# Merging two work streams on a NeuronCore: the hand-out tables of all four compute engines replaced

## What is computed

```python
x = x + ssm(layernorm(x))     # gated state-space layer, 8 heads, with a rotation of the state
x = x + ffn(layernorm(x))     # 256 -> 2 x 1024 -> 1024 -> 1024 -> 256
x = x + delta(layernorm(x))   # delta-rule attention, 8 heads of 32, scan over the tokens
x = x + ffn(layernorm(x))     # the same weights as the first

def ffn(x):
    h = silu((x @ w1.T) * s1) * ((x @ w2.T) * s2)
    h = gelu((h @ h1.T) * sh1)
    h = gelu((h @ h2.T) * sh2)
    return (h @ w3.T) * s3
```

## Time and profile before

| | us |
|---|---|
| median of 3 runs | 2490.34 |
| lowest and highest run | 2489.7, 2496.93 |
| the profiled execution | 2494.62 |
| its span in the trace | 2492.6 |

### The profile page before, as it was taken

One profiled execution on the slowest core, in us unless ns is written; L12 is line 12 of the kernel. 1 busy time (PEld: TensorE's weight loads), 2 busy tenths in 40 slices (PEclk: granted clock), 3 DMA queues, 4 the chain that ended last, 5 costly groups with the idle time before them and its releaser, 6 DMA issues.

```text
span 2492.6 us, 60186 instructions
## 1 busy us (share of the span) xinstructions
PE 2245.7 (90%) x24704; PEld 1963.5 (79%) x24704; DVE 1221.2 (49%) x3186; ACT 1102.8 (44%) x2169; POOL 804.7 (32%) x873
## 2 busy tenths in 40 slices
PE   5798985897999989999999989999899999899888
PEld 3577974676888878887788878888798888888788
DVE  4546344455635654355534656346543655434431
ACT  3465431363435733365333654356342664333233
POOL 3222331322333233332333333332332333233233
PEclk8799997898999999999999999999999999999999
DMA  8000001000010001000010000100010000000000
GB/s 258 1 1 1 1 6 29 4 1 3 17 36 2 1 11 39 7 1 2 19 34 4 1 2 18 36 2 1 7 40 10 1 1 18 25 4 19 18 11 9
DMA packets 85456, 43.69 MB, mean 18 GB/s; under 512 B 69936, under 2 KB 80048, under 8 KB 85168
## 3 DMA queue, kind: packets, MB, share of 16 engines
q1 hardware_dynamic: 81504, 28.11, 4.6%
q0 software_dynamic: 3664, 11.53, 1.4%
HBM read 27.05 MB, written 12.58 MB: 16 GB/s over the span
## 4 chain that ended last, share of the span: by engine, by line
PE 55%; issue 16%; DVE 14%; POOL 9%; ACT 3%; DMA 1%; SPq 0%; DVEq 0%; POOLq 0%; ACTq 0%
PE F L1336 23%; PE Q L1395 5%; PE F L1315 5%; POOL hA_lo L604 4%; PE Q L1465 2%; PE F L1358 2%; PE Q L1429 2%; DVE hid L976 2%; POOL hB_lo L604 2%; PE Q L1448 2%; POOL rn L660 2%; DVE Q L1176 2%; DVE ti L1178 2%; PE Q L1433 1%; PE Q L1407 1%
## 5 line engine op out<-in xcount | busy, mean ns | idle before, releaser
L604 POOL TENSOR_TENSOR hA_lo<-hid,hA_hi 128x512 fp32r<-128x512 f32 x256 | 333.4, 1303 | 660.4 <-ACT hA_hi L741 348.0
L1336 PE MATMUL F<-hB_hi,h_sb 128*128 128x256 f32 x2048 | 499.7, 286 | 6.4 <-POOL hB_lo L604 6.4
L1336 PE MATMUL F<-hA_hi,h_sb 128*128 128x256 f32 x2048 | 500.8, 287 | 4.2 <-POOL hA_lo L604 4.2
L1336 PE MATMUL F<-hA_lo,h_sb 128*128 128x256 f32 x2048 | 487.5, 280 | 4.8 <-issue 4.8
L1336 PE MATMUL F<-hB_lo,h_sb 128*128 128x256 f32 x2048 | 488.4, 280 | 0.0
L1336 PEld LDWEIGHTS F<-hB_hi,h_sb 128*128 128x128 f32 x2048 | 387.2, 189 | 16.1 <-POOL hB_lo L604 8.8
L1336 PEld LDWEIGHTS F<-hA_hi,h_sb 128*128 128x128 f32 x2048 | 386.5, 189 | 13.2 <-POOL hA_lo L604 6.4
L1336 PEld LDWEIGHTS F<-hA_lo,h_sb 128*128 128x128 f32 x2048 | 387.1, 189 | 6.9 <-issue 6.6
L1336 PEld LDWEIGHTS F<-hB_lo,h_sb 128*128 128x128 f32 x2048 | 387.9, 189 | 0.0
L1315 PE MATMUL F<-xf_hi,w_sb 128*128 128x256 f32 x1024 | 275.3, 305 | 39.3 <-DVEq L980 21.0
L737 ACT ACTIVATE hid<-F,sh_sb 128x256 f32<-128x256 f32 x256 | 121.7, 475 | 392.2 <-PE F L1336 382.7
(11 more groups left out here) (199 smaller groups left out, 3953.8 us busy)
## 6 DMA issues: line engine op xcount, KB each, us to landing
h_sb<-h_dram POOLq DMA_DIRECT2D x2, 4096.0 KB, 23.8
x_sb<-x_dram SPq DMA_DIRECT2D x8, 512.0 KB, 5.5
a_scr<-amv SPq DMA_DIRECT2D x32, 128.0 KB, 2.3
au<-a_scr SPq DMA_DIRECT2D x8, 512.0 KB, 3.2
t_scr<-ti SPq DMA_DIRECT2D x8, 512.0 KB, 2.6
tbd<-t_scr SPq DMA_DIRECT2D x128, 32.0 KB, 1.9
out_dram<-x_sb SPq DMA_DIRECT2D x8, 512.0 KB, 3.0
w_sb<-w_dram POOLq DMA_DIRECT2D x3, 1024.0 KB, 7.8
```

The source lines that it names most:

```text
L604: pool.tensor_tensor(lo, hid[:, n % 2], hi.bitcast(F32), ALU.subtract).then_inc(f_lo.handle, 1)
L1336: last = pe.matmul(ps[:, i * TOK:(i + 1) * TOK], w[:, k, o:o + P], part[:, k, :], start=(i == 0 and k == 0 and part is src[0]), stop=(i == ...
```

## The change

Only the strings of the five plans change, 20 tables in all: for each window one for PE, ACT, DVE and POOL. No instruction of either stream is added or taken away by the text of the kernel; the code below the tables is the same. The diff, cut to the PE tables, the BODY table of ACT and the LAST table of DVE (the others are replaced in the same way):

```diff
 FIRST_PLAN = {
-    "pe": ("0 0 0 0 0 0 0 0 0 0 0 0 0 0 0 0 0 0 0 0 0 0 0 0 0 1 0 1 1 1 2 0 2 0 0 1 1 2 0 1 0 0 0 0 0 0 3 0 "
-             "3 0 2 0 0 1 2 2 0 2 0 0 0 1 1 3 4 5 0 7 1 2 6 3 21"),
...
+    "pe": ("0 0 0 0 0 0 0 0 0 0 0 0 0 0 0 0 0 0 0 0 0 0 0 0 0 0 1 0 4 0 2 0 0 0 0 2 0 3 0 2 0 0 0 1 1 2 2 0 "
+             "1 0 0 0 0 2 0 2 0 0 2 2 0 0 3 4 8 1 5 0 1 2 6 16 7"),
...
 }
 PEEL_PLAN = {
-    "pe": ("2 0 0 2 0 1 0 0 0 0 1 1 2 5 0 0 8 0 0 0 0 0 0 0 0 0 0 0 0 0 0 0 0 0 0 0 0 1 0 0 0 0 0 0 3 0 0 0 "
-             "0 0 1 4 1 0 1 4 3 0 2 0 2 0 0 0 1 0 3 0 0 0 1 0 0 0 0 2 0 0 1 0 0 0 0 0 0 0 0 0 0 0 2 0 0"),
...
+    "pe": ("2 0 0 1 0 0 0 1 0 1 0 3 0 2 0 1 10 0 0 0 1 0 0 0 0 0 0 0 0 0 0 0 1 0 0 0 0 0 0 0 0 0 0 0 0 1 1 "
+             "1 2 2 1 1 2 0 1 2 3 0 0 3 1 0 1 0 0 0 2 0 0 0 0 0 0 1 0 2 0 0 0 0 0 0 0 0 2 0 0 0 1 0 1 0 0"),
...
 }
 BODY_PLAN = {
-    "pe": ("2 0 3 0 0 1 1 0 0 0 1 1 0 0 2 1 32 1 0 0 1 0 0 0 0 1 0 1 0 0 2 1 1 0 0 3 2 1 0 0 2 0 2 0 0 2 1 "
-             "0 0 0 1 2 1 2 1 2 3 1 0 8 2 0 0 0 2 0 4 0 1 0 0 1 0 2 0 3 0 0 0 0 0 0 1 0 3 0 1 0 0 1 1 0 0"),
-    "act": ("2 0 2 0 2 0 0 2 0 0 0 0 4 17 0 1 3 5 4 0 5 2 0 4 2 0 2 0 0 0 2 1 0 0 0 0 1 1 0 1 0 1 0 0 0 0 1 "
-             "0 0 0 0 2 0 0 1 0 0 0"),
...
+    "pe": ("2 0 1 2 0 0 0 2 0 0 2 0 0 2 0 1 32 1 1 1 1 0 1 0 0 1 1 0 0 0 1 0 1 0 0 3 1 1 0 0 1 2 1 0 0 3 1 "
+             "1 0 0 1 1 1 0 2 2 3 1 0 8 2 0 1 0 2 1 3 0 1 0 0 0 0 1 0 4 0 0 0 0 0 0 1 0 3 0 0 0 0 1 2 0 0"),
+    "act": ("2 0 1 3 0 0 0 0 2 0 0 1 3 17 2 1 1 4 5 0 5 2 0 2 4 2 0 0 0 0 2 1 1 0 0 0 0 1 0 0 1 0 1 0 0 0 0 "
+             "0 0 1 1 0 0 0 0 1 1 0"),
...
 }
 LATE_PLAN = {
-    "pe": ("1 1 2 1 1 1 0 2 0 3 0 1 0 1 1 2 27 0 0 0 1 1 0 1 1 0 0 1 0 0 0 0 1 0 2 0 1 1 1 0 1 0 2 0 1 2 3 "
-             "1 0 0 2 1 0 0 2 5 6"),
...
+    "pe": ("2 0 2 1 1 1 2 0 0 2 0 0 1 2 2 1 30 0 0 1 1 1 0 0 0 0 1 1 0 0 0 0 1 0 0 1 1 1 0 0 1 1 0 0 0 3 2 "
+             "1 1 1 1 1 1 1 1 1 9"),
...
 }
 LAST_PLAN = {
-    "pe": ("3 1 3 0 1 2 0 0 0 2 0 0 0 2 1 0 26 1 0 0 1 0 0 0 0 0 0 3 0 0 0 0 1 0 0 0 0 0 0 0 1 0 0 0 0 2 0 "
-             "0 0 0 0 0 2 0 1 0 1"),
...
-    "dve": ("2 3 1 2 0 0 0 2 0 0 0 0 0 2 0 0 0 0 1 0 0 0 0 0 0 0 1 0 2 0 0 0 0 0 2 3 2 2 0 1 0 0 0 0 0 0 0 0 "
-             "0 0 0 0 0 1 0 1 0 0 0 0 2 0 0 0 1 0 0 1 0 0 0 0 0 0 0 0 2 0 0 0 0 0 0 2 0"),
...
+    "pe": ("3 1 2 1 1 2 0 1 0 2 0 0 0 0 2 1 29 1 0 0 0 0 1 0 0 0 0 0 0 0 0 0 0 0 0 1 0 0 0 0 0 0 0 0 0 2 0 "
+             "0 1 0 0 0 1 0 1 0 1"),
...
+    "dve": ("5 0 4 1 0 1 1 0 0 0 2 0 1 0 0 0 0 0 0 1 0 0 0 0 0 1 0 1 3 1 4 0 0 0 0 0 0 0 2 0 0 1 0 0 0 0 0 0 "
+             "0 0 0 0 0 1 0 0 0 0 0 0 0 0 1 0 0 0 0 0 0 0 0 0 1 0 1 0 0 1 0 0 1 0 0 1 0"),
...
 }
```

## The result

The changed kernel took 2455.56 us (median of 4 runs, 2450.81 to 2458.52) beside 2493.64 us for the kernel before (4 runs, 2489.7 to 2501.45): a ratio of 0.9842, interval 0.981 to 0.9873.

> The changed kernel again, beside the next three. Ratio to before 0.984 as on record; its start-up up to sums of tile 3 between 91 and 96 us.

What follows compares the result with a forecast made beforehand. PE's stream, matmul work plus waits from its own order, bounds the kernel. Window gains 9.0 + 11.2 + 5.1 + 3.8 + 2.8 = 31.9 us, cut to 19, give median 2471 us; range 2460 to 2482, widened to 2455 to 2492.

Steps and rivals of the forecast that it cites:

- The discount: Whole sum: every step covering one wait uncovers another place, so six tenths of 31.9 us, 19 us, is gained.
- rival B: FIRST and PEEL: fewer waits also give back a quarter of the half-clock time, 8 us more, 2463 us; chance 0.11.
- that of the walk: Walks: uncovered neighbours cost 0.34 us each; gains PEEL 1.4, BODY 5.1, LATE 1.7 us, loss LAST 0.7.
- FIRST, 9.0 counted: FIRST: FFN cover moves to four waits of 3.52, 1.66, 2.55 and 1.27 us; all covered gives 9.0 us.
- PEEL, 11.2 counted: PEEL: gains at uw0 3.7, seg of tile 0 3.2, seg of tile 3 2.9, walk 1.4; together 11.2 us.
- The term for uw0 (3.7): PEEL: inversion chain ends 6.1 us earlier, 2.4 us of work moves later; 3.7 gained, 12.6 of 16.34 wait stays.
- BODY, 5.1 counted: BODY: nothing large moves; three fewer uncovered walk neighbours a turn give 5.1 us; added table loads cost nothing.
- LATE, 3.8 counted: LATE: five fewer uncovered neighbours give 1.7 us, and the 2.08 us wait for DVE's gated product goes; together 3.8.
- LAST, 2.8 counted: LAST: transposes' 3.47 us wait for xnf goes, two more uncovered neighbours cost 0.7; gain 2.8 us.
- C: LAST's walk, with 20 uncovered neighbours, falls to the half clock, costing 18 us: 2499 us, slower; chance 0.08.
- D: The 25 added table loads reach PE at 1.28 us each, 32 us: 2503 us, slower; chance 0.05.
- A: Whole kernel: the waits only move; 0 to 7 us gained, 2487 us; chance 0.20.

Runs made afterwards that it cites:

- the moved steps of the experiment: Changed kernel with three FFN steps (52 matmuls) moved from PEEL's walk to ahead of uw0: 2452.58 us, ratio 0.9833.
- everything together: Changed kernel with three FFN steps moved and 50 unread matmuls ahead of uw0 in PEEL, 512-column fillers in PEEL's and LAST's walks: 2452.11 us, 0.983.

## Why the prediction was wrong

- **The discount.** The step that failed is the last of the sum, "I take six tenths, 19 us". By the table of means PE's idle time fell by 28.8 us and not by 19, which is nine tenths of the full count of 31.9. Another 7.2 us came from PE's busy time, which the sum had put at nothing and left to rival B; B's mechanism, priced at 8 us more, thus came on top. Together that is 36.1 us in the traces and 38 to 41 in the timing. The argument was that FFN work is fixed, so a covered wait uncovers another. That holds step by step (L1485 and L1475, the new 4.18 us, the moved steps of the experiment), but not in the total: an FFN step covers a wait only if it stands beside one, and the old order had cover at places that needed none.
- **Luck in the full count.** That it was near the truth is in part luck, since its terms missed both ways. In FIRST and PEEL, where the scans are short of cover, idle time fell by 4.3 and 8.1 us of 9.0 and 11.2 counted, five to seven tenths, much as the discount had it. In BODY and LATE it fell by 9.5 and 5.1 of 5.1 and 3.8 counted, more than all. The one term that held by its mechanism is that of the walk: the neighbours without cover were counted at 1.4 + 5.1 + 1.7 - 0.7 = 7.5 us over all windows, and the waits for DVE's ur and st fell by 6.9.
- **FIRST, 9.0 counted, 11.5 measured.** By another way: some 4 us of idle time stayed won, 4 to 8 came from the busy time at a higher clock (0.96 to 0.98 instead of 0.95 behind sums of tile 3), and 1.3 of the mean are the spread of the start.
- **PEEL, 11.2 counted, 12.2 measured.** The term for uw0 (3.7) failed: its wait rose to 19.0 instead of falling to 12.6. A wait for POOL that stood between gram and uw0 in the kernel before

```profile
388.30 0.58 PE L1336 MATMUL F<-hB_hi,h_sb 128*128 128x256 f32 x1 [3.59 <-POOL hB_lo L604]
```

went, and its time reappears at uw0, since the inversion chain and not PE's order sets when uw0 can start. That chain starts at gram of tile 3, which came 42.4 us after the window's begin in all four old traces and 37.2 to 41.7, on average 3.3 us earlier, in the five new ones, not the 6.1 counted; and from there to uw0 it took 37.9 to 38.2 us before and 39.4 to 39.7 after, for a reason that was not followed up. So uw0 came 80.3 to 80.6 us after the window's begin before and 76.8 to 81.1 after, 1.8 us earlier on average. The walk gained 1.9 us on average (65.1 to 61.2 in the traces shown, but the other old ones have 62.2 to 63.3), for 1.4 counted. The SSM part behind it was counted at 3.2 + 2.9 = 6.1 and gained 8.5: seg of tile 0 no longer waits, that of tile 3 0.59 instead of 5.51. The new wait at sums that I deducted is not at tile 0 but at tile 1 (1.67).
- **BODY, 5.1 counted, 5.3 in the lengths, 9.5 in idle time, 10.0 in the timing.** The walk's term was right (11.9 to 7.0 us of waits for ur and st over the five turns), but "nothing large moves" left out as much again of small waits elsewhere: those for DVE's y at its transposes and for ACT ahead of FFN steps went, and others came, fewer in sum. PE's busy time rose by 4.2 us, 0.9 of it the step from LATE. The rest goes with the granted clock, 0.994 before and 0.993 after on average, but four old traces cannot tell it from spread. The loads cost nothing, as costed.
- **LATE, 3.8 counted, 6.9 measured.** Idle time went from 14.4 to 9.3 us: the waits for L980 fell from 3.3 us in all to 0.7, with none above 0.3 left, where before had 2.08 and others. 0.9 us is the step that now falls in BODY, and 0.9 is busy time at a granted clock of 1.00 instead of 0.99.
- **LAST, 2.8 counted, 0.3 measured.** The wait of 3.47 us for xnf is gone. The clock in the walk took 0.7 to 3.6 us back, depending on the execution, and the waits for the gated product (L980) rose from 4.2 to 5.1 us over the window.
- **C** was half right: the clock fell under 0.9 in LAST's walk. I priced it at 18 us, by laying PEEL's walk beside LAST's; but with fillers PEEL's walk still takes 57.05 us at 0.94 of the clock, and only FFN steps pay for the clock. The price is 3.6 us at most. **D** is out, and **A** too, as a statement on the total.

Of the signs I had named, PE idle in PEEL (48.8), in FIRST (50.0), in BODY (14.9 to 16.4 a turn), the xnf wait, seg of SSM tile 0 and the 257 loads came as written; uw0's wait, sums of that tile and PE's busy time in BODY (278.31 in the first turn at a clock of 0.98, against 273.6 to 275.4 in the others) did not. Of the signs of being wrong, PE's idle time stayed below 242 us, but a walk outside PEEL did fall below 0.9, that of LAST.

## What to carry to other kernels

When two streams are merged by hand, count the waits that a new order covers and check for each whether its cover came from a place that was waiting too. Here half to seven tenths of the count stayed where nearly every step waits (FIRST, PEEL), and all of it, with some small waits that were not counted, where most places have cover to spare (BODY, LATE). A low clock costs only where PE has work queued: before pricing it, split the stretch into work that PE sets the pace of and work that another engine's chain sets. Cover ahead of a long chain's end shortens the wait on the books but not the time at which the chain ends; only an earlier start or a shorter chain does that.

## What the runs showed of the hardware

The granted clock of LAST's walk was 0.82 in three traces in which no wait in the walk was longer than 0.52 us, and 0.89 in the two of the changed kernel, which have one wait of 0.74 us; the waits between the groups of small matmuls are 0.3 to 0.5 us. The old order, with 18 neighbours that have nothing between them instead of 20 and 180 FFN matmuls in the walk instead of 116, had 1.00 in three of its four traces and 0.97 in the fourth. With an unread bf16 matmul of 256 columns after every ws and sp it was 1.00, at no cost in the chain, and with one of 128 columns 0.96. Each of these is one trace, and with 512 columns it was 1.00 in one kernel and 0.96 in another (everything together), so the step from 128 to 256 columns is not shown to matter. The same steps up to sums of tile 3 took 90 to 96 us from one execution to the next, so a difference of 5 us between two single traces of FIRST says nothing. A table load took 1.283 us with the next activation right behind it, and 32 more of them did not show in the time.
